# Sixteen-channel attention in a two-layer decoder: another order for the products of the row maximum

## The chip, the cores and the metric

The kernel runs on one core of one Trainium2 chip, as one program. The metric is the device time of one launch in microseconds (us), the median of three runs.

## The reference

The program is a whole two-layer decoder on x of shape (4, 512, 256), with a context of shape (4, 1601, 256). The change is in the second layer's cross attention alone: 16 heads of 16 channels, full softmax over 1601 keys, no mask.

```python
q = _split_heads(Q @ W_q.T + b_q)
k = _split_heads(K @ W_k.T + b_k)
v = _split_heads(V @ W_v.T + b_v)
scores = jnp.einsum('bhqd,bhkd->bhqk', q, k) / jnp.sqrt(jnp.float32(D_K))
probs = jax.nn.softmax(scores, axis=-1)
ctx = jnp.einsum('bhqk,bhkd->bhqd', probs, v)
```

## The kernel before

The function is `full_attention` (line 1577). One *unit* is a batch b and a group g of four heads, 16 units in all, numbered u = 4b + g. The four heads j of a group lie in four quarters of the partitions, 32 rows each (16 channels, one row for the maximum, the rest zero). So a product of head j uses only rows 32j to 32j+31 of TensorE's array, its *quarter*.

For each unit the softmax's maximum is found first. It takes 64 *chunks*: a chunk (line 1845) is one product of 128 queries by 400 keys of one head, written to one of three PSUM banks, the *ring*. VectorE reads it (line 1753) into one column of row maxima and so frees the bank (`ring_free`). After the last chunk `row_max` folds the columns and negates them into `less`; TensorE turns `less` (line 1852), VectorE adds it to the queries (`shift`, line 1766), so that the scores come out with the maximum taken off.

Then the unit is worked through in 13 *slots*, one for each tile of 128 keys. In slot s TensorE does, in its written order, the score products of tile s+1 (line 1866, one for each head, 512 queries wide, each waits until ScalarE has taken the bank's last exponential) and the *output* products of tile s (line 1877, four heads in four column strips). ScalarE does the exponentials (line 1715). The 64 chunks of the *next* unit are spread over slots 0 to 10 (`chunks_of`: 5, 6, 6, 6, 6, 5, 6, 6, 6, 6, 6). The first four of a slot are interleaved with the four score products (score 0, chunk, score 1, chunk, ...), the others follow. `chunk_at` gives chunk i the head i % 4. The sets thus begin on heads 0, 1, 3, 1, 3, 1, 2, 0, 2, 0, 2 in slots 0 to 10. So in slots 0, 7 and 9 every score product stands beside a chunk of its own head.

The ring also takes other work, in the order that `take` writes down and that all engines follow:
- a *piece*: one part of the next batch's Q, K or V (lines 1825 to 1832, two products over all 128 rows, each in two passes), taken by VectorE (lines 1741 to 1747). Each batch has 33, in slots 0 to 12 of the units with g = 1 and 2 and slots 0 to 6 of those with g = 3, for the first three batches. The piece stands after the slot's chunks and ahead of the output products.
- *sums*, in slot 1: the product that adds up and spreads the softmax's denominators of the unit before (line 1885). VectorE takes its reciprocal (line 1770) and scales the unit's output with it (line 1772).
- *out*, in slots 4 and 5 after the last group of a batch: the output projection (line 1894), added to x by VectorE (line 1777).

A TensorE instruction that needs a bank waits until the use three turns before has been read (`await_bank`).

Of the kernel before, what the change touches and what calls it, by code (L numbers as in the profile page):

```python
# [27 lines left out]
TB = T // P  # L28
S2 = 1601
KT = -(-S2 // P)  # L30
# [1516 lines left out]
FJ = P // FQ  # L1547
# [4 lines left out]
NKB = len(KB)  # L1552
# [24 lines left out]
def full_attention(nc, c):  # L1577
# [4 lines left out]
    SCALE = float(FD) ** -0.5  # L1582
    UNITS = [(b, g) for b in range(B) for g in range(FG)]
    LAST_UNIT = len(UNITS) - 1
    CHUNKS = FJ * TB * NKB
    MAX_SLOTS = KT - 2
    LESS_SLOT, SUMS_SLOT, OUT_SLOTS = KT - 2, 1, (4, 5)
    RING = 3
    with Scope(nc, "fa") as s:
# [48 lines left out]

        def chunks_of(slot):

            return range(CHUNKS * min(slot, MAX_SLOTS) // MAX_SLOTS, CHUNKS * min(slot + 1, MAX_SLOTS) // MAX_SLOTS)

        def first_chunks(n):

            rest = len(PIECES) - FIRST
            return range(CHUNKS * n // rest, CHUNKS * (n + 1) // rest)

        def chunk_at(i):

            return i % FJ, i // FJ // NKB, i // FJ % NKB  # L1650

        def piece_of(u, slot):

            b, g = UNITS[u]
            n = (g - 1) * KT + slot
            return n if b + 1 < B and g >= 1 and n < len(PIECES) else None
# [6 lines left out]
        def take(*use):  # L1663
            turn[use] = len(turn)
# [5 lines left out]
        take("less", 0)  # L1670
        for u, (b, g) in enumerate(UNITS):
            for slot in range(KT):
                for i in chunks_of(slot) if u < LAST_UNIT else ():
                    take("chunk", u + 1, i)
                if slot == LESS_SLOT and u < LAST_UNIT:
                    take("less", u + 1)
                if piece_of(u, slot) is not None:
                    take("piece", b + 1, piece_of(u, slot))
                if slot == SUMS_SLOT and u:
                    take("sums", u - 1)  # L1680
                if slot in OUT_SLOTS and u and ends(u - 1):
                    take("out", b - 1, OUT_SLOTS.index(slot))
# [47 lines left out]
        @block.vector  # L1730
        def _(dve):
            def await_turn(*use):
                dve.wait_ge(ring_ready, turn[use] + 1)

            def piece(b, n):
                what, g, m = PIECES[n]
                await_turn("piece", b, n)
                src = bank("piece", b, n)
                if what == "V":
                    rows = keys(m)  # L1740
                    ins = nc.vector.tensor_tensor(V[0:rows, b % 2, m, :, 0:FD], src[0:rows, 0:D].rearrange("p (h d) -> p h d", d=FD),
                                                  bv[0:rows, :].rearrange("p (h d) -> p h d", d=FD), ALU.add)
                elif what == "Q":
                    ins = nc.vector.tensor_scalar(Q[:, b % 2, g, :], src[:], bqk[:, 0, g:g + 1], None, ALU.add)
                else:
                    k0, w = KEYS[m]
                    ins = nc.vector.tensor_scalar(K[:, b % 2, g, k0:k0 + w], src[:, 0:w], bqk[:, 1, g:g + 1], None, ALU.add)
                ins.then_inc(ring_free, 1)

            def chunk(u, i):  # L1750
                j, t, n = chunk_at(i)
                await_turn("chunk", u, i)
                nc.vector.tensor_reduce(part[:, t, j, n:n + 1], bank("chunk", u, i)[:, 0:KB[n][1]], AX, ALU.max  # L1753
                                        ).then_inc(ring_free, 1)

            def row_max(u):
                dve.wait_ge(ring_free, turn["chunk", u, CHUNKS - 1] + 1)
                nc.vector.tensor_reduce(top[:].rearrange("p t j -> p (t j)"), part[:].rearrange("p t j n -> p (t j) n"), AX, ALU.max
                                        ).then_inc(top_ready, 1)
                dve.wait_ge(top_ready, u + 1)  # L1760
                nc.vector.tensor_scalar(less[:, :, :, DEN], top[:], -1.0, None, ALU.mult).then_inc(less_ready, 1)

            def shift(u):
                b, g = UNITS[u]
                await_turn("less", u)
                nc.vector.tensor_tensor(Qm[:, u % 2, :], bank("less", u)[:], Q[:, b % 2, g, :], ALU.add).then_inc(ring_free, 1)

            def scale(u):
                await_turn("sums", u)
                nc.vector.reciprocal(share[:], bank("sums", u)[:]).then_inc(ring_free, 1)  # L1770
                dve.wait_ge(ring_free, turn["sums", u] + 1)
                nc.vector.tensor_tensor(att[:, UNITS[u][1], :], raw[:], share[:], ALU.mult).then_inc(att_ready, 1)

            def add_output(b, half):
                rows = c.x[:, b * TB + half * 2:b * TB + half * 2 + 2, :]
                await_turn("out", b, half)
                nc.vector.tensor_tensor(rows, rows, bank("out", b, half)[:].rearrange("p (t d) -> p t d", d=D), ALU.add
                                        ).then_inc(ring_free, 1)

            nc.vector.memset(pv[:], 0.0).then_inc(made, 1)  # L1780
            dve.wait_ge(loaded, LOADS)
            dve.wait_ge(made, MADE)
            for n in range(len(PIECES)):
                piece(0, n)
                for i in first_chunks(n - FIRST) if n >= FIRST else ():
                    chunk(0, i)
            row_max(0)
            shift(0)
            dve.wait_ge(based, 1)
            for u, (b, g) in enumerate(UNITS):  # L1790
                for slot in range(KT):
                    if u < LAST_UNIT:
                        for i in chunks_of(slot):
                            chunk(u + 1, i)
                        if slot == MAX_SLOTS - 1:
                            row_max(u + 1)
                        if slot == LESS_SLOT:
                            shift(u + 1)
                    if piece_of(u, slot) is not None:
                        piece(b + 1, piece_of(u, slot))  # L1800
                    if slot == SUMS_SLOT and u:
                        scale(u - 1)
                    if slot in OUT_SLOTS and u and ends(u - 1):
                        add_output(b - 1, OUT_SLOTS.index(slot))
            scale(LAST_UNIT)
            for half in range(2):
                add_output(B - 1, half)

        @block.tensor
        def _(pe):  # L1810
# [45 lines left out]
            def scores(u, kt, j):  # L1856

                b, g = UNITS[u]
                n = keys(kt)
                at = (u * KT + kt) * FJ + j  # L1860
                if kt == 0 and j == 0:
                    pe.wait_ge(ring_free, turn["less", u] + 1)
                if at >= FJ:
                    pe.wait_ge(p_ready, at - FJ + 1)
                rows = slice(j * FQ, (j + 1) * FQ)
                nc.tensor.matmul(sps[j][0:n, :], K[rows, b % 2, g, kt * P:kt * P + n], Qm[rows, u % 2, :],  # L1866
                                 start=True, stop=True).then_inc(s_ready, 1)
# [38 lines left out]
                scores(0, 0, j)  # L1906
            for u, (b, g) in enumerate(UNITS):
                for slot in range(KT):
                    ahead = list(chunks_of(slot)) if u < LAST_UNIT else []
                    nxt = (u, slot + 1) if slot + 1 < KT else (u + 1, 0) if u < LAST_UNIT else None  # L1910
                    for j in range(FJ):
                        if nxt and nxt != (u + 1, 0):
                            scores(*nxt, j)
                        if j < len(ahead):
                            chunk(u + 1, ahead[j])
                    for i in ahead[FJ:]:
                        chunk(u + 1, i)
                    if slot == LESS_SLOT and u < LAST_UNIT:
                        turn_less(u + 1)
                    if piece_of(u, slot) is not None:  # L1920
                        piece(b + 1, piece_of(u, slot))
                    if nxt == (u + 1, 0):
                        for j in range(FJ):
                            scores(*nxt, j)
                    if slot == SUMS_SLOT and u:
                        add_up(u - 1)
                    if slot in OUT_SLOTS and u and ends(u - 1):
                        out_product(b - 1, OUT_SLOTS.index(slot))
                    output(u, slot)
            add_up(LAST_UNIT)  # L1930
            for half in range(2):
                out_product(B - 1, half)
# [1209 lines left out]
```

## Time and profile before

| | us |
|---|---|
| median of three runs | 8619.73 |
| lowest and highest | 8613.97, 8625.38 |
| profiled execution, device time | 8617.03 |
| its span | 8615.2 |
| main loop of `full_attention` in it | 1134.30 |
| TensorE busy in the loop | 1097.03 |
| VectorE, ScalarE busy in the loop | 635.78, 446.33 |

The span is the time from the first to the last instruction that the profiler saw; the device time lies 1.8 us above. Busy times of engines overlap. Products in different quarters run beside each other, and their ends are modelled, so a busy TensorE is not one at its limit.

### The profile page before, as it was taken

What the parts mean: (1) busy time and instruction counts of PE and PEld (TensorE: products, weight loads), DVE (VectorE), ACT (ScalarE), POOL (GpSimd) and SP (SyncE); (2) the same over time, 40 slices, a digit from 0 to 9 for tenths busy, and PEclk for the clock granted to TensorE, in tenths of its full rate; (3) what the DMA queues carried; (4) which work ended last, traced back from release to release, by engine and by line L of the source; (5) the groups of instructions that cost most, each with busy time, mean ns of one, the idle gap of its engine ahead of it and who ended that gap; (6) DMA issues with size and microseconds to landing.
All of it is one profiled execution on the core that took longest, in us unless ns stands there. A gap on an engine that the chain in (4) does not pass through costs nothing. (4 is left out here: it accounts for less than half of the span.)

```text
span 8615.2 us, 102487 instructions
## 1 busy us (share of the span) xinstructions
PE 7109.9 (83%) x35402; PEld 4802.5 (56%) x35402; DVE 4861.0 (56%) x7898; ACT 2854.5 (33%) x5165; POOL 711.7 (8%) x695
## 2 busy tenths in 40 slices
PE   6887887887879888888888889956653899999799
PEld 4775766756757666666666744422222334333577
DVE  5656655656646666666666610058886555555621
ACT  3223222232224444444444411134441233334210
POOL 0111111111100000000000000023333000000000
PEclk8998998998989999999999999978886899999895
DMA  0000000000000000000000010000000000000110
GB/s 33 0 1 1 0 1 1 0 1 1 0 33 9 7 20 9 7 20 7 8 19 9 7 55 0 0 18 0 0 0 3 26 8 1 8 1 1 40 49 10
DMA packets 23873, 89.02 MB, mean 10 GB/s; under 512 B 5784, under 2 KB 9120, under 8 KB 18480
## 3 DMA queue, kind: packets, MB, share of 16 engines
q1 hardware_dynamic: 23456, 83.53, 2.8%
q8 instruction: 253, 4.15, 0.2%
q14 instruction: 164, 1.34, 0.1%
HBM read 81.43 MB, written 2.10 MB: 10 GB/s over the span
## 5 line engine op out<-in xcount | busy, mean ns | idle before, releaser
L1252 DVE TENSOR_TENSOR xa_PT<-xa_tps,xa_PT 128x512 fp32r<-128x512 f32 (+1 forms) x1024 | 555.3, 584 | 386.0 <-ACT xa_PT L1127 382.3
L1753 DVE TENSOR_REDUCE fa_part<-fa_ring 128x1 f32<-128x400 f32 (+1 forms) x1024 | 533.0, 569 | 330.2 <-PE fa_ring L1845 312.3
L1715 ACT ACTIVATE fa_prob<-fa_sps 128x512 f32<-128x512 f32 (+1 forms) x832 | 439.9, 601 | 782.8 <-PE fa_sps L1866 774.1
L635 DVE TENSOR_TENSOR gdn_XX<-gdn_XX,gdn_wps 128x512 f32<-128x512 f32 (+1 forms) x768 | 477.2, 640 | 367.8 <-PE gdn_wps L799 360.1
L496 ACT ACTIVATE gdn_Y<-gdn_yps 128x256 f32<-128x256 f32 x768 | 295.2, 384 | 1051.6 <-PE gdn_yps L784 1045.2
L1405 PE MATMUL xa_tps<-ident,xa_prob 128*128 128x128 f32 (+1 forms) x3328 | 501.4, 284 | 162.3 <-DVE xa_PT L1252 161.6
L1845 PE MATMUL fa_ring<-fa_K,fa_Q 32*128 32x400 f32 (+1 forms) x2048 | 586.6, 546 | 36.7 <-DVE fa_part L1753 23.5
L1405 PEld LDWEIGHTS xa_tps<-ident,xa_prob 128*128 128x128 f32 (+1 forms) x3328 | 393.1, 143 | 388.6 <-DVE xa_PT L1252 317.7
L1127 ACT ACTIVATE xa_PT<-xa_tps 128x512 fp32r<-128x512 f32 (+1 forms) x1024 | 471.2, 514 | 416.1 <-PE xa_tps L1405 415.9
L796 PE MATMUL gdn_wps<-gdn_Y,gdn_XX 128*128 128x128 f32 x3072 | 601.2, 287 | 2.9
L1240 DVE CUSTOM_DVE_ANT_0 xa_prob<-xa_sps,xa_mask 128x1604 f32<-128x1604 f32 x256 | 467.4, 1826 | 130.0 <-PE xa_sps L1387 123.4
L796 PEld LDWEIGHTS gdn_wps<-gdn_Y,gdn_XX 128*128 128x128 f32 x3072 | 472.9, 196 | 67.4 <-issue 35.9
L1115 ACT ACTIVATE xa_prob<-xa_prob,xa_neg 128x1604 f32<-128x1604 f32 x256 | 418.2, 1634 | 268.2 <-DVE xa_neg L1243 268.1
L799 PE MATMUL gdn_wps<-gdn_XX,gdn_Y 128*128 128x128 f32 x2560 | 503.5, 279 | 0.0
L1387 PE MATMUL xa_sps<-xa_K,xa_Q 128*128 128x402 f32 x2048 | 466.7, 372 | 29.6 <-issue 16.9
L1423 PE MATMUL xa_pv<-xa_PT,xa_V 128*128 128x256 f32 (+1 forms) x3328 | 453.4, 292 | 11.1 <-DVE xa_PT L1252 11.1
L2042 PE MATMUL ffn_mid<-ffn_hid,ffn_h 128*128 128x512 f32 x1024 | 441.5, 593 | 9.7 <-DVE ffn_hid L2008 6.3
L1423 PEld LDWEIGHTS xa_pv<-xa_PT,xa_V 128*128 128x128 f32 (+1 forms) x3328 | 415.9, 189 | 49.2 <-issue 28.8
L2361 DVE TENSOR_TENSOR_SCAN scan_h<-scan_dA,scan_dBx 128x2048 f32<-128x2048 f32 x64 | 407.8, 6372 | 26.4 <-POOL scan_dBx L2235 20.2
L1387 PEld LDWEIGHTS xa_sps<-xa_K,xa_Q 128*128 128x128 f32 x2048 | 382.7, 198 | 45.1 <-issue 36.0
L799 PEld LDWEIGHTS gdn_wps<-gdn_XX,gdn_Y 128*128 128x128 f32 x2560 | 398.5, 196 | 0.0
L1845 PEld LDWEIGHTS fa_ring<-fa_K,fa_Q 32*128 32x128 f32 x2048 | 245.9, 187 | 270.9 <-DVE fa_part L1753 222.2
(424 smaller groups left out, 12365.8 us busy)
## 6 DMA issues: line engine op xcount, KB each, us to landing
xa_wqk<-in_xa_wqk SPq DMA_DIRECT2D x64, 256.0 KB, 2.6
moe_own_w<-in_moe_w SPq DMA_DIRECT2D x14, 1024.0 KB
ffn_h<-in_ffn_h SPq DMA_DIRECT2D x2, 4096.0 KB, 27.5
xa_ctxT<-in_ctxT SPq DMA_DIRECT2D x4, 1601.0 KB
fa_ctxT<-in_ctxT SPq DMA_DIRECT2D x4, 1601.0 KB
xa_mask<-in_mask SPq DMA_DIRECT2D x4, 802.0 KB, 9.0
ffn_w<-in_ffn_w SPq DMA_DIRECT2D x3, 1024.0 KB, 18.1
x<-in_x SPq DMA_DIRECT2D x1, 2048.0 KB
```

Of the source, the lines that this page charges most:

```text
L635: nc.vector.tensor_tensor(X[:, half, 0:n], X[:, half, 0:n], wps[half][:, 0:n], ALU.subtract).then_inc(X_ready, 1)
L796: last = nc.tensor.matmul(wps[half][:, 0, e, :], X[:, half, 1, e, :], Y[:, h, :], start=True, stop=True)
L799: last = nc.tensor.matmul(wps[half][:, 1, e, :], Y[:, h, :], X[:, half, 1, e, :], start=True, stop=True)
L1127: nc.scalar.activation(PT[0:n, u // 2 % NPT, 0, k0:k1, u % 2, :], turned_bank(u, g)[0:n, 0:k1 - k0, :], ACT.Copy).then_inc(t_hi, 1)
L1240: nc.vector.tensor_tensor_reduce(parts(prob[:, e, :]), sps[:, :, 0:SW], parts(mask[:, u % TB if masked else 0, :]), 1.0, -3.0e38, ALU.add, ...
L1252: nc.vector.tensor_tensor(PT[0:n, u // 2 % NPT, 1, k0:k1, u % 2, :], turned_bank(u, g)[0:n, 0:k1 - k0, :], PT[0:n, u // 2 % NPT, 0, k0:k1, ...
L1387: last = nc.tensor.matmul(sps[:, n, 0:SWW], Q[:, hh % 2, e, q * P:(q + 1) * P], k, start=(e == 0), stop=(e == 1))
L1405: last = nc.tensor.transpose(turned_bank(u, g)[0:n, kt - k0, :], prob[:, u % 2, kt * P:kt * P + n], c.ident[:])
L1423: nc.tensor.matmul(pv[0:MV, 0:2 * P], V[0:n, kt, hh].rearrange("p e d -> p (e d)"), PT[0:n, pair % NPT, part, kt].rearrange("p a q -> p (a ...
L1753: nc.vector.tensor_reduce(part[:, t, j, n:n + 1], bank("chunk", u, i)[:, 0:KB[n][1]], AX, ALU.max).then_inc(ring_free, 1)
L1845: nc.tensor.matmul(bank("chunk", u, i)[:, 0:w], Q[rows, b % 2, g, t * P:(t + 1) * P], K[rows, b % 2, g, k0:k0 + w], start=True, stop=True) ...
L2042: last = nc.tensor.matmul(mid[m % 2][:], w[n][:, k, m * P:(m + 1) * P], hid[e][:, k, :], start=(k == 0), stop=(k == MH - 1))
```

## The change

The 64 chunks of a unit are shared out in whole sets of four: `chunks_of` gives 4, 4, 8, 4, 8, 4, 8, 4, 8, 4, 8 chunks to slots 0 to 10, split in an early part (four) and a late part (four or none). `chunk_at` begins each set at head 2. In a slot with a late part TensorE's order becomes: scores and early chunks interleaved, `less`, piece, late chunks, sums or out, output. In a slot without one: scores and early chunks, `less`, piece, output, sums or out. VectorE and the order of the ring follow. The row maximum is taken after slot 10's late part.

```diff
+    QUADS = TB * NKB
+    CHUNKS = FJ * QUADS
...
         def chunks_of(slot):
-            return range(CHUNKS * min(slot, MAX_SLOTS) // MAX_SLOTS, CHUNKS * min(slot + 1, MAX_SLOTS) // MAX_SLOTS)
+            first, last = (QUADS * min(n, MAX_SLOTS) // MAX_SLOTS * FJ for n in (slot, slot + 1))
+            return range(first, min(first + FJ, last)), range(first + FJ, last)
...
         def chunk_at(i):
-            return i % FJ, i // FJ // NKB, i // FJ % NKB
+            return (i + FJ // 2) % FJ, i // FJ // NKB, i // FJ % NKB
...
@@ the ring's order (VectorE's loop is changed in the same way) @@
-                for i in chunks_of(slot) if u < LAST_UNIT else ():
+                early, late = chunks_of(slot) if u < LAST_UNIT else ((), ())
+                for i in early:
                     take("chunk", u + 1, i)
                 if slot == LESS_SLOT and u < LAST_UNIT:
                     take("less", u + 1)
                 if piece_of(u, slot) is not None:
                     take("piece", b + 1, piece_of(u, slot))
+                for i in late:
+                    take("chunk", u + 1, i)
...
@@ TensorE @@
-                    ahead = list(chunks_of(slot)) if u < LAST_UNIT else []
-                    nxt = (u, slot + 1) if slot + 1 < KT else (u + 1, 0) if u < LAST_UNIT else None
+                    early, late = chunks_of(slot) if u < LAST_UNIT else ((), ())
                     for j in range(FJ):
-                        if nxt and nxt != (u + 1, 0):
-                            scores(*nxt, j)
-                        if j < len(ahead):
-                            chunk(u + 1, ahead[j])
-                    for i in ahead[FJ:]:
-                        chunk(u + 1, i)
+                        if slot + 1 < KT:
+                            scores(u, slot + 1, j)
+                        if j < len(early):
+                            chunk(u + 1, early[j])
                     if slot == LESS_SLOT and u < LAST_UNIT:
                         turn_less(u + 1)
                     if piece_of(u, slot) is not None:
                         piece(b + 1, piece_of(u, slot))
-                    if nxt == (u + 1, 0):
+                    if slot + 1 == KT and u < LAST_UNIT:
                         for j in range(FJ):
-                            scores(*nxt, j)
+                            scores(u + 1, 0, j)
+                    if not late:
+                        output(u, slot)
+                    for i in late:
+                        chunk(u + 1, i)
                     if slot == SUMS_SLOT and u:
                         add_up(u - 1)
                     if slot in OUT_SLOTS and u and ends(u - 1):
                         out_product(b - 1, OUT_SLOTS.index(slot))
-                    output(u, slot)
+                    if late:
+                        output(u, slot)
```

## Rows read from the trace of the kernel before

**Rows 1.** Part 5 of the page: costliest groups; busy, mean of one, idle before.
```profile
L1845 PE MATMUL fa_ring<-fa_K,fa_Q 32*128 32x400 f32 (+1 forms) x2048 | 586.6, 546 | 36.7 <-DVE fa_part L1753 23.5
```

**Rows 2.** Windows: stretch, us, each engine's busy time, PEclk; the main loop.
```profile
6803.60:7937.90 1134.30, 1097.03 (x5826) 435.78 (x5830) 635.78 (x1140) 446.33 (x847) 0.00 (x0) 0.97 0.01 4
```

**Rows 3.** Waits in the loop: who for whom, us in total, times, longest.
```profile
PEld fa_ring L1845 <- DVE fa_part L1753: 212.6, 462, 1.3
...
PEld fa_pv L1877 <- ACT fa_prob L1715: 30.5, 51, 0.8
```

**Rows 4.** Windows: slots 3, 4, 5, 6 and 7 of unit 0.
```profile
6825.44:6830.28 4.84, 4.84 (x34) 1.76 (x30) 3.17 (x6) 2.17 (x4) 0.00 (x0) 1.00 0.01 3
6830.28:6835.07 4.79, 4.76 (x34) 1.99 (x30) 3.18 (x6) 2.06 (x4) 0.00 (x0) 1.00 0.00 0
6835.07:6839.42 4.35, 4.35 (x31) 1.46 (x27) 2.69 (x5) 2.17 (x4) 0.00 (x0) 1.00 0.00 0
6839.42:6844.06 4.64, 4.62 (x33) 1.95 (x29) 3.08 (x6) 2.06 (x4) 0.00 (x0) 1.00 0.00 0
6844.06:6849.33 5.27, 4.63 (x33) 1.77 (x29) 3.08 (x6) 2.17 (x4) 0.00 (x0) 1.00 0.00 0
```

**Rows 5.** Timeline: slot 6 of unit 4 (quarter 2), then slot 7's first read.
```profile
7144.75 0.18 PEld L1866 LDWEIGHTS fa_sps<-fa_Qm,fa_K 32*128 32x128 f32 x1 [0.85 <-issue]
...
7145.95 0.57 DVE L1753 TENSOR_REDUCE fa_part<-fa_ring 128x1 f32<-128x401 f32 x1 [1.39 <-PE fa_ring L1845]
7146.44 0.57 DVE L1753 TENSOR_REDUCE fa_part<-fa_ring 128x1 f32<-128x401 f32 x1
7146.58 0.29 PEld L1845 LDWEIGHTS fa_ring<-fa_K,fa_Q 32*128 32x128 f32 x2 [0.68 <-DVE fa_part L1753]
...
7147.54 0.29 PEld L1845 LDWEIGHTS fa_ring<-fa_K,fa_Q 32*128 32x128 f32 x2 [0.19 <-DVE fa_part L1753]
7147.55 0.57 DVE L1753 TENSOR_REDUCE fa_part<-fa_ring 128x1 f32<-128x400 f32 x1
7148.41 0.13 PEld L1877 LDWEIGHTS fa_pv<-fa_prob,fa_V 128*17 128x17 f32 x8 [0.57 <-ACT fa_prob L1715]
7149.39 0.33 PEld L1866 LDWEIGHTS fa_sps<-fa_Qm,fa_K 32*128 32x128 f32 x8 [0.85 <-issue]
...
7151.22 3.14 DVE L1753 TENSOR_REDUCE fa_part<-fa_ring 128x1 f32<-128x400 f32 x6 [2.13 <-PE fa_ring L1845]
```

**Rows 6.** Windows: six chunks on quarter 2 with a V, K, last-K piece.
```profile
7214.80:7220.50 5.70, 5.68 (x37) 2.63 (x33) 3.50 (x7) 2.06 (x4) 0.00 (x0) 1.00 0.00 0
7292.53:7299.08 6.55, 6.53 (x37) 2.63 (x33) 3.83 (x7) 2.06 (x4) 0.00 (x0) 1.00 0.00 0
7074.35:7079.58 5.23, 5.21 (x37) 2.48 (x33) 3.36 (x7) 2.07 (x4) 0.00 (x0) 1.00 0.00 0
```

**Rows 7.** Windows of slot 1 (units 4 and 5); timeline: reciprocal in unit 4, slot 2.
```profile
7109.43:7115.32 5.89, 5.88 (x36) 2.05 (x32) 4.05 (x7) 2.17 (x4) 0.00 (x0) 1.00 0.00 0
7181.17:7188.78 7.61, 7.61 (x40) 2.81 (x37) 4.81 (x8) 2.17 (x4) 0.00 (x0) 1.00 0.00 0
...
7114.44 3.36 DVE L1770 RECIPROCAL fa_share<-fa_ring 128x512 f32<-128x512 f32 x1 [0.48 <-PE fa_ring L1885]
7115.31 0.18 PEld L1866 LDWEIGHTS fa_sps<-fa_Qm,fa_K 32*128 32x128 f32 x1 [0.85 <-issue]
...
7117.85 0.60 PE L1845 MATMUL fa_ring<-fa_K,fa_Q 32*128 32x400 f32 x1 [0.74 <-DVE fa_share L1770]
```

**Rows 8.** Windows: slot 2 (units 5, 6), slots 7, 9 (unit 5), slots 2-3 (unit 13).
```profile
7188.78:7197.25 8.47, 7.64 (x38) 2.67 (x34) 6.90 (x9) 2.17 (x4) 0.00 (x0) 1.00 0.00 0
7265.34:7274.56 9.22, 8.39 (x38) 3.20 (x34) 6.58 (x9) 2.17 (x4) 0.00 (x0) 0.81 0.00 0
7220.50:7226.84 6.34, 5.70 (x38) 2.45 (x34) 3.50 (x7) 2.17 (x4) 0.00 (x0) 1.00 0.00 0
7232.54:7240.46 7.92, 7.28 (x38) 2.96 (x34) 3.53 (x7) 2.17 (x4) 0.00 (x0) 0.78 0.00 0
7785.93:7800.14 14.21, 13.38 (x63) 4.86 (x59) 9.32 (x14) 4.34 (x8) 0.00 (x0) 0.76 0.00 0
```

More of the change, by code:

```diff
@@ L1584, in full_attention @@
     LAST_UNIT = len(UNITS) - 1
-    CHUNKS = FJ * TB * NKB
+    QUADS = TB * NKB
+    CHUNKS = FJ * QUADS
     MAX_SLOTS = KT - 2
@@ L1791, in _ @@
                 for slot in range(KT):
-                    if u < LAST_UNIT:
-                        for i in chunks_of(slot):
-                            chunk(u + 1, i)
[L1795 to L1798, printed above, removed]
+                    early, late = chunks_of(slot) if u < LAST_UNIT else ((), ())
+                    for i in early:
+                        chunk(u + 1, i)
+                    if slot == LESS_SLOT and u < LAST_UNIT:
+                        shift(u + 1)
                     if piece_of(u, slot) is not None:
                         piece(b + 1, piece_of(u, slot))
+                    for i in late:
+                        chunk(u + 1, i)
+                    if slot == MAX_SLOTS - 1 and u < LAST_UNIT:
+                        row_max(u + 1)
                     if slot == SUMS_SLOT and u:
@@ L1908, in _ @@
                 for slot in range(KT):
-                    ahead = list(chunks_of(slot)) if u < LAST_UNIT else []
-                    nxt = (u, slot + 1) if slot + 1 < KT else (u + 1, 0) if u < LAST_UNIT else None
+                    early, late = chunks_of(slot) if u < LAST_UNIT else ((), ())
                     for j in range(FJ):
-                        if nxt and nxt != (u + 1, 0):
-                            scores(*nxt, j)
-                        if j < len(ahead):
-                            chunk(u + 1, ahead[j])
-                    for i in ahead[FJ:]:
-                        chunk(u + 1, i)
+                        if slot + 1 < KT:
+                            scores(u, slot + 1, j)
+                        if j < len(early):
+                            chunk(u + 1, early[j])
                     if slot == LESS_SLOT and u < LAST_UNIT:
@@ L1921, in _ @@
                         piece(b + 1, piece_of(u, slot))
-                    if nxt == (u + 1, 0):
+                    if slot + 1 == KT and u < LAST_UNIT:
                         for j in range(FJ):
-                            scores(*nxt, j)
+                            scores(u + 1, 0, j)
+                    if not late:
+                        output(u, slot)
+                    for i in late:
+                        chunk(u + 1, i)
                     if slot == SUMS_SLOT and u:
```

## The prediction

> **What bounds the kernel now.** I read the costliest groups first [rows 1]: the products for the maximum (L1845, "chunks") keep TensorE for 587 us. Most of them lie in the stage's main loop, 1134 us of the span at a clock of 0.97, with VectorE busy for 636 and ScalarE for 446 [rows 2]. All parts below are about that loop, since little else is edited. Its waits [rows 3] say who sets the pace: loads of chunks wait 213 us for a read (L1753) to free one of three banks, and the output products wait only 31 us for ScalarE. So neither TensorE's speed nor ScalarE's decides; it is the loop chunk, read, free bank, next chunk.
>
> A unit has 13 slots. I count slot s from its first score product (that of tile s+1) to the next slot's. [Rows 4] are slots 3 to 7 of unit 0, which have no pieces: six chunks that begin on quarter 1 take 4.84, on quarter 3 4.79, five on quarter 1 4.35, six on quarter 2 4.64, six on quarter 0 5.27. Each chunk less is 0.49 (4.84 less 4.35). Quarter 2 is the best start, quarter 0 the worst, as there score product and chunk of the same quarter stand side by side: the first read begins at 1.83 us (7151.22 less 7149.39) instead of 1.20 (7145.95 less 7144.75) [rows 5].
>
> **The slots of the new order.** Every set now begins on quarter 2. The set of the interleaved four is then exactly what slot 6 of unit 4 had [rows 5], and I build from that slot: reads at 1.20, 1.69 and, the fourth, 2.80; the fourth chunk at 1.83, 0.63 after the first read's start, as it needs its bank; its read 0.97 after it; output products 0.87 after the last chunk's start (7148.41 less 7147.54); next slot 0.98 after these. Three chunks thus cost 0.63 + 0.97 = 1.60 us, where reads alone would be 1.45.
> - Four chunks: 1.83 + 0.87 + 0.98 = 3.68 us. Slots 0, 1, 3, 5, 7, 9.
> - Eight chunks: fourth read 2.80, fifth 3.29, so the eighth chunk at 3.29 + 0.63 = 3.92, output at 4.78, total 5.76. Slots 2, 4, 6, 8, 10.
> A pair is 9.44 against 9.28 for two sixes on quarter 2: the uneven sets cost 0.16 a pair, the better start pays for it.
>
> **A unit without pieces**, change by slot: 0 (was five on quarter 0, 5.27 less one chunk, 4.79): -1.11. 3: -1.16. 4: +0.97. 5: -0.68. 6, 8, 10: +1.12 each. 7, 9: -1.59 each. Together -1.80. Slots 1 and 2 hold the sums: before, product of the sums, then output; now output, then product. Slot 1 was 5.89 [rows 7], becomes 3.68 + 1.05 (the product: 5.89 less 4.84) = 4.73, -1.16. But the reciprocal (3.36 us [rows 7]) began 0.87 before slot 2 (7114.44 against 7115.31) (1.16 after its product, which stood 1.05 + 0.98 before slot 2); the product now stands 1.05 before slot 2, so it begins 0.11 into the slot. It is 0.98 later; all that hangs on it in slot 2, the third chunk and the fourth score product behind it (at 7117.85 now), is 0.98 later too. Slot 2 at full clock was 6.56 (8.47 in unit 5 with a 1.91 piece [rows 8]), and two chunks more are 1.12: 8.66, +2.10. The unit comes to **-0.86 us**; 14 units (1 to 14) make -12.0. Unit 0 has no sums and a slow start: its slots by the same prices give -2.0. Unit 15 has no chunks: 0. The output projections in slots 4 and 5 keep their 3.65 us.
>
> **Pieces.** A piece added 1.06 (V), 1.91 (K of 512, Q) or 0.59 us (last K) to a six-chunk slot on quarter 2 (the windows less 4.64) [rows 6]. In four-chunk slots this stays. In eight-chunk slots the piece now stands after the fourth chunk: it can start at 2.70 (0.87 after a chunk), where the fifth chunk would have started at 2.32. So everything later is late by the piece's length and 0.38 more. 39 pieces are in such slots (five in each of units 1, 2, 5, 6, 9, 10, three in 3, 7, 11): +14.8. In slot 1 piece and sums no longer stand together; before that saved 0.2 us (7.61 [rows 7] for 5.89 + 1.91): nine units, +1.8. VectorE's reads of a piece lie beside TensorE. The row maximum after slot 10 comes 1.12 us later in a slot that is 1.12 longer: 0. The first units' chunks before the loop only change quarter by rotation: 0. ctxT's load has 70 us until it is wanted: 0.
>
> The Trainium skill has a rule that speaks against this change: "Changing tiling mode (not just tile) drains the TensorE" (TensorEngine Tiling (Array Packing), Key Properties). The trace agrees in that a product over all rows starts 0.87 us after a chunk where a chunk on another quarter starts 0.48 after it (two in 0.96, 7146.58 to 7147.54) [rows 5]; without the rule the 14.8 us above would be nought.
>
> At full clock the sum is -12.0 - 2.0 + 14.8 + 1.8 = **+2.6 us**.
>
> **The clock.** Asked slot by slot, the clock falls to its lower level (1.2 GHz) at 14 places in units 1 to 14, for a few us each; [rows 8] hold three of them and two slots without. Nine are in slot 2, after TensorE's pause for the reciprocal; five in slots 7 and 9, which begin on quarter 0 and leave TensorE idle for 0.64 us (6.34 less 5.70). Eleven are short: slot 2 with V 9.22 where 6.56 + 1.06 = 7.62 is due, slot 9 with V 7.92 where slot 7 has 6.34, 1.6 us each. Three are long (units 1, 13, 14): slots 2 and 3 of unit 13 take 14.21 for 6.56 + 4.84, 2.8 us. Together 26 us, 8 of them in slots 7 and 9. Those five should go: -8. In slot 2 the pause before the third chunk grows from 0.74 [rows 7] to 1.7 us. In the five units there without a piece (4, 8, 12, 13, 14) it fell each time (3 x 1.6 + 2 x 2.8 = 10.4); I expect that again with one more of the long kind: 11.6. In the nine with a piece it fell in four (3 x 1.6 + 2.8 = 7.6); I expect five: 9.2. So +3. Bounds: it falls nowhere, -26 in all; in slot 2 of all 14 units at 2.8 us, 39 in place of 26, +13. Estimate: **-5 us**.
>
> In all 2.6 - 5 = -2 us. The profiled execution took 8617.03 (span 8615.2 and 1.8 around it): 8615 by it. The median of three is 8619.73, 2.7 above, so I say **8618 us**.
>
> **Rivals.**
> 1. *Clock falls in the sets of eight* (ends slower). From 1.83 to 4.78 us of such a slot TensorE does one chunk after another, each on a quarter of its rows, longer than now (1.83 to 3.66). If that is thin enough for the clock to fall, each fall costs 1.6 us; there are 75 such slots, 36 of them without a piece between. One in three of the 75: 25 x 1.6 = 40, 8658 us. It decides from 12 falls on (19 us on the -2). For it: slots 7 and 9 fell with three chunks after a pause. Against: they had a 0.65 us standstill, the new ones have none, and no slot on quarter 2 fell. 12%.
> 2. *Later reciprocal lowers the clock in every unit*: the bound above, +13, and +2.6: +16; with 0.6 us more in each where the slow stretch reaches further into slot 3, +24: 8635 to 8643. 8%.
> 3. *Falls nearly all go*, since no slot has same-quarter neighbours and the sets are denser: -26 + 2.6 = -23, 8596. Against it: the longer pause in slot 2. 9%.
> 4. *The mode change is paid on both sides of a split-off piece*: another 14.8 us on the -2, 8633. Against: V's 1.06 us in a slot already holds its way out into another mode [rows 6]. By the skill's rule on the mode this would be the drain back into the quarters. 4%.
> 5. *The change doesn't do what it says*: neighbours used other quarters already in slots 2, 4, 6, 8 and 10, so little is left to win; that is in the sum, and if the gain of 1.59 us in slots 7 and 9 did not come, 14 x 3.2 = 45 us slower. The rows of both starts stand side by side, so 2%.
>
> **How the numbers follow.** My forecast has 65%, the rivals 35%. Its own range is 8606 to 8630: the clock term by 8 us either way and the slot prices by 0.03 us over 154 slots, some 5 us. With rivals the range is 8596 to 8643. By 0.2% (17 us, about what a measurement tells from none): faster, below 8602.5, rival 3 and a tail: 0.12. Slower, above 8637, rivals 1 and 5, part of 2 and a tail: 0.18. Within: 0.70.
>
> **What would show it.** Four-chunk slots without a piece at 3.68 us and eight-chunk ones at 5.76; slot 8 with V 7.20 and with K 8.05; the reciprocal beginning 0.1 us inside slot 2 and slot 2 at 8.7 us or, with a fallen clock, near 10; stage within 10 us of 1134; clock full in slots 7 and 9 of units 1, 5, 9. Wrong if eight-chunk slots show a clock below 1, or if they take over 6.2 us at full clock.

## The result: 0.6% slower, and the profile after

The changed kernel takes 8675.29 us (8671.07 to 8678.64, 4 runs) against 8622.56 us for the kernel before in the same runs. The ratio is 1.0063, 95% interval 1.0047 to 1.0078. The forecast was 8618 us with a range of 8596 to 8643 us, so it was wrong, and on the side of rivals 1 and 2. One execution of a later experiment, e5_filler (10431 us), and one of the kernel before beside it (12307 us) ran at a lower clock from end to end and are left out of every median and ratio below.

In the code of after, chunks are at L1852, their reads at L1758, score products at L1873 and the reciprocal at L1775. The group of part 5 that answers to [rows 1]; its products are the same 2048, and 109 us longer:

```profile
L1852 PE MATMUL fa_ring<-fa_K,fa_Q 32*128 32x400 f32 (+1 forms) x2048 | 695.8, 581 | 30.1 <-DVE fa_share L1775 24.1
```

Waits in the loop, as [rows 3]. Chunks wait less for a free bank than before (175 for 213 us), so the waits for a bank, on which the prediction built, are not what grew:

```profile
PEld fa_ring L1852 <- DVE fa_part L1758: 174.8, 345, 1.3
```

Windows of after (stretch, us, busy PE, PEld, DVE, ACT, POOL, then PEclk): the loop, answering to [rows 2], and units 1 to 14; slots 7 and 8 of unit 7 (four and eight chunks); slot 8 of unit 5 (eight, V) and of unit 6 (eight, K), answering to [rows 6]; slots 1, 2 and 3 of unit 4 [rows 7]; slot 9 of unit 5 [rows 8]; slot 10 of unit 13.

```profile
6812.40:7995.30 1182.90, 1152.16 (x5806) 455.72 (x5806) 641.08 (x1140) 435.26 (x841) 0.00 (x0) 0.92 0.01 4
6875.19:7963.00 1087.81, 1057.95 (x5284) 420.60 (x5280) 602.58 (x1071) 384.30 (x744) 0.00 (x0) 0.92 0.01 4
7415.03:7418.71 3.68, 3.66 (x28) 1.37 (x24) 2.11 (x4) 2.06 (x4) 0.00 (x0) 1.00 0.61 255
7418.71:7424.48 5.77, 5.75 (x36) 2.54 (x32) 4.14 (x8) 2.06 (x4) 0.00 (x0) 1.00 0.00 0
7254.40:7261.61 7.21, 7.11 (x40) 2.93 (x36) 4.65 (x9) 2.06 (x4) 0.00 (x0) 1.00 0.01 2
7335.98:7344.04 8.06, 8.04 (x40) 2.94 (x36) 4.98 (x9) 2.06 (x4) 0.00 (x0) 1.00 0.00 0
7126.85:7131.58 4.73, 4.71 (x30) 1.67 (x26) 2.11 (x4) 2.07 (x4) 0.00 (x0) 1.00 0.00 0
7131.58:7142.62 11.04, 9.24 (x33) 3.57 (x32) 8.09 (x10) 2.17 (x4) 0.00 (x0) 0.72 0.00 0
7142.62:7147.82 5.20, 5.20 (x28) 2.33 (x24) 2.21 (x4) 2.17 (x4) 0.00 (x0) 0.62 0.00 0
7261.61:7266.35 4.74, 4.72 (x32) 2.05 (x28) 2.54 (x5) 2.07 (x4) 0.00 (x0) 1.00 0.00 0
7889.29:7895.91 6.62, 6.60 (x36) 2.56 (x32) 4.54 (x10) 2.06 (x4) 0.00 (x0) 0.87 0.00 0
```

Two things are to be seen. Where PEclk is 1.00 the slots have the lengths that were forecast: 3.68, 5.77 (for 5.76), 7.21 (7.20), 8.06 (8.05), 4.73. And the loop's clock is 0.92 where it was 0.97: slots 2 and 3 of unit 4 are at 0.72 and 0.62, and slot 10 of unit 13, eight chunks without a piece, takes 6.62 at 0.87. The prediction had named a clock below 1 in such a slot as a sign that it is wrong. There TensorE does one chunk after another and then the output products, which take 1.91 us where those of the slot before took 1.05:

```profile
7888.33 1.05 PE L1884 MATMUL fa_pv<-fa_prob,fa_V 128*17 128x512 f32 x8
...
7890.61 3.55 PE L1852 MATMUL fa_ring<-fa_K,fa_Q 32*128 32x400 f32 x11
7894.09 1.91 PE L1884 MATMUL fa_pv<-fa_prob,fa_V 128*17 128x512 f32 x8
```

The window of the loop (its first line above, 1182.90 us) ends where the last tile's score products start; to that point the loop of the kernel before took 1130.7 us. So it grew by 52 us, as much as the medians differ (53). The two profiled executions differ by 60 us; the other 8 lie ahead of the loop, in code that is the same in both. Slot 2 of unit 4 in the timeline (start, us, engine, line):

```profile
7131.71 3.36 DVE L1775 RECIPROCAL fa_share<-fa_ring 128x512 f32<-128x512 f32 x1 [1.47 <-PE fa_ring L1892]
...
7135.13 0.60 PE L1852 MATMUL fa_ring<-fa_K,fa_Q 32*128 32x400 f32 x1 [1.72 <-DVE fa_share L1775]
...
7136.34 1.03 PE L1852 MATMUL fa_ring<-fa_K,fa_Q 32*128 32x400 f32 x1
```

The reciprocal begins 0.13 us into the slot (forecast 0.11), TensorE stands still for 1.72 us for it (0.74 before, [rows 7]), and 1.2 us later a pass of a chunk (each product is done in two) takes 1.03 us in place of 0.60: the lower level of the clock.

### The profile page after: what moved, and what is told of

The parts are those of the page before. It is cut to its first block and busy times, and to the rows that moved or that the text cites. A ratio compares the mean times of both kernels' runs of the same rounds, so it can differ in the third digit from the quotient of the medians.

```text
span 8675.6 us, 102487 instructions
## 1 busy us (share of the span) xinstructions
PE 7171.4 (83%) x35402; PEld 4821.7 (56%) x35402; DVE 4867.6 (56%) x7898; ACT 2846.4 (33%) x5165; POOL 710.8 (8%) x695
## 5 line engine op out<-in xcount | busy, mean ns | idle before, releaser
L1758 DVE TENSOR_REDUCE fa_part<-fa_ring 128x1 f32<-128x400 f32 (+1 forms) x1024 | 538.3, 570 | 343.6 <-PE fa_ring L1852 327.1
L1852 PE MATMUL fa_ring<-fa_K,fa_Q 32*128 32x400 f32 (+1 forms) x2048 | 695.8, 581 | 30.1 <-DVE fa_share L1775 24.1
L1387 PE MATMUL xa_sps<-xa_K,xa_Q 128*128 128x402 f32 x2048 | 465.1, 371 | 29.6 <-issue 16.9
L1852 PEld LDWEIGHTS fa_ring<-fa_K,fa_Q 32*128 32x128 f32 x2048 | 270.2, 198 | 262.6 <-DVE fa_part L1758 184.4
L1873 PE MATMUL fa_sps<-fa_Qm,fa_K 32*128 32x512 f32 (+1 forms) x1664 | 412.6, 668 | 1.5 <-DVE fa_Qm L1771 0.8
## 6 DMA issues: line engine op xcount, KB each, us to landing
moe_own_w<-in_moe_w SPq DMA_DIRECT2D x14, 1024.0 KB
ffn_w<-in_ffn_w SPq DMA_DIRECT2D x3, 1024.0 KB, 18.1
```

The lines of the kernel that those rows point to most:

```text
L1387: last = nc.tensor.matmul(sps[:, n, 0:SWW], Q[:, hh % 2, e, q * P:(q + 1) * P], k, start=(e == 0), stop=(e == 1))
L1852: nc.tensor.matmul(bank("chunk", u, i)[:, 0:w], Q[rows, b % 2, g, t * P:(t + 1) * P], K[rows, b % 2, g, k0:k0 + w], start=True, stop=True) ...
```

## How each kernel is split into slots and clock

For units 1 to 14, a *full-clock sum* can be made for every kernel from the slot prices of the prediction: 154 slots, plus slots 11 and 12 as they are (2.59 and 2.65 without a piece). What the measured stretch has above it is what the clock cost. I split that into slots 2 and 3 and the rest, and count the places where the clock falls, by the slot in which it falls. "Still" is TensorE's standstill in slot 2, "behind" the chunks that follow it there one by one before the output (in the five units without a piece; with one, after and e1 have one chunk, the piece and then four), "most" the largest set in slots 4 to 10. Full-clock sums, clock and falls are for units 1 to 14 of the one profiled execution of each kernel. That of e5 is the fastest of its runs (8607.01 us), that of e9 the slowest (8541.42). Still, what the stretch gains or loses against the kernel before agrees with the ratios within 10 us.

| kernel | ratio to before (95%) | units 1-14 | full clock | clock, slots 2-3 | clock, rest | falls slot 2 / rest | still, behind, most |
|---|---|---|---|---|---|---|---|
| before | 1 | 1035.5 | 1008.5 | 18.8 | 8.2 | 9 / 5 | 0.74, 3, 6 |
| after | 1.0063 (1.0047-1.0078) | 1087.8 | 1013.1 | 49.9 | 24.9 | 14 / 12 | 1.72, 5, 8 |
| e1_sums_first | 1.0029 (1.0019-1.0040) | 1067.6 | 997.5 | 40.5 | 29.6 | 12 / 13 | 0.74, 5, 8 |
| e2_before_sums_late | 1.0038 (1.0024-1.0051) | 1068.9 | 1024.0 | 36.8 | 8.1 | 14 / 5 | 1.72, 3, 6 |
| e3_quarter_two | 0.9948 (0.9935-0.9962) | 993.8 | 971.6 | 21.9 | 0.3 | 9 / 0 | 0.74, 3, 6 |
| e4_piece_last | 1.0023 (1.0014-1.0032) | 1057.5 | 982.7 | 40.5 | 34.3 | 14 / 19 | 0.74, 5, 8 |
| e5_filler | 1.0003 (0.9994-1.0013) | 1033.8 | 1013.1 | 4.8 | 16.0 | 3 / 10 | filled, 5, 8 |
| e6_q2_filler | 0.9925 (0.9912-0.9938) | 971.9 | 971.6 | 0.0 | 0.2 | 0 / 0 | filled, 3, 6 |
| e7_sevens | 0.9987 (0.9979-0.9996) | 1033.1 | 980.6 | 35.2 | 17.3 | 13 / 10 | 0.74, 4, 7 |
| e8_slot2_four | 0.9939 (0.9927-0.9952) | 988.2 | 971.6 | 16.4 | 0.3 | 8 / 0 | 0.74, 1, 6 |
| e9_split | 0.9884 (0.9868-0.9901) | 945.0 | 944.7 | 0.1 | 0.2 | 0 / 0 | none, -, 6 |

In unit 0, which the table leaves out, the clock falls in slots 2, 6 and 10 of after, e1, e4 and e5. The others have no fall in it after the low clock with which every kernel's loop begins. (The 21 falls of e4 that the expectation of e7 names take in those of slots 6 and 10.)

e6 and e9, in which the clock never falls, meet their sums within 0.3 us in 972 and 945: the prices can be trusted to split the others.

The window of units 1 to 14 of the kernel before, against which the fences below are read:

```profile
6866.51:7902.00 1035.49, 1000.41 (x5286) 400.48 (x5282) 597.28 (x1071) 391.64 (x744) 0.00 (x0) 0.97 0.01 4
```

## The experiments

Theory A: the reciprocal begins later, TensorE stands still longer in slot 2, the clock falls. Theory B: the sets of eight lower it, chunk after chunk, each on a quarter of the rows. Of kernels e1 to e4 the lines shown are units 1 to 14.

**e1_sums_first**: after, with the sums' product ahead of the output again.

```diff
-                    if not late:
+                    if not late and slot != SUMS_SLOT:
                         output(u, slot)
...
-                    if late:
+                    if late or slot == SUMS_SLOT:
                         output(u, slot)
```

> The changed kernel with one edit taken back: in slot 1 the product of the sums stands ahead of the output products again. Full-clock prices of its slots against the kernel before: +4.6 us (the changed kernel) - 14 x 0.98 (reciprocal earlier) - 1.8 (piece and sums together again) = -11. Theory A (the reciprocal that begins 0.98 us later lengthens TensorE's pause in slot 2, and that lowers the clock there): the clock's cost goes back to about that of the kernel before less its 8 us in slots 7 and 9, so 8600 to 8612 us, and slots 2 and 3 together lose under 25 us to the clock instead of 50. Theory B (the sets of eight, chunk after chunk on a quarter of the rows, are what lowers it): the clock still costs 35 us or more above the kernel before, 8640 to 8655 us.

8643.69 us (8640.02 to 8653.13, before 8615.47).

```profile
6870.17:7937.81 1067.64, 1051.07 (x5286) 418.09 (x5282) 602.78 (x1071) 384.39 (x744) 0.00 (x0) 0.92 0.01 4
```

In units 1 to 14 it wins back 20 us, and 15.6 of them are slot prices. The clock still costs 70 us, and 12 falls stay in slot 2: theory B's figure. By the ratios e1 is 29 us faster than after, so the later reciprocal is 5 us (these two traces) to 14 us (the ratios) of the clock's cost, a small part as long as the sets of eight stand.

**e2_before_sums_late**: before, with that edit alone.

```diff
-                    if slot == SUMS_SLOT and u:
-                        add_up(u - 1)
+                    if slot == SUMS_SLOT:
+                        output(u, slot)
+                        if u:
+                            add_up(u - 1)
```

> The kernel before with this one edit done alone: in slot 1 the output products stand ahead of the product of the sums. Full-clock prices: 14 x 0.98 + 1.8 = +15.5 us. Theory A: the clock falls in slot 2 of nearly all 14 units and costs 15 to 25 us more, 8650 to 8663 us. Theory B: the clock costs what it did, 8635 to 8640 us.

8650.78 us (8643.80 to 8654.58).

```profile
6862.13:7931.03 1068.90, 1020.58 (x5286) 409.26 (x5282) 597.86 (x1071) 391.66 (x744) 0.00 (x0) 0.95 0.01 4
```

The full-clock sum is 15.5 us more, the clock costs 18 us more in slots 2 and 3, and it falls there in all 14 units: theory A. So the later sums lower the clock without sets of eight, and the sets of eight lower it without the later sums (e1). The two overlap in slot 2.

**e3_quarter_two**: before, sets of five and six kept, each begun on head 2.

```diff
+        HEADS, rest = [], 0
+        for slot in range(MAX_SLOTS):
+            n = len(chunks_of(slot))
+            HEADS += [(k + FJ // 2) % FJ for k in range(FJ)] + [(rest + k + FJ // 2) % FJ for k in range(n - FJ)]
+            rest += n - FJ
+        NTH = [HEADS[:i].count(j) for i, j in enumerate(HEADS)]
         def chunk_at(i):
-            return i % FJ, i // FJ // NKB, i // FJ % NKB
+            return HEADS[i], NTH[i] // NKB, NTH[i] % NKB
```

> The kernel before with its five or six chunks a slot, only the heads of each slot's set are chosen so that every set begins on head 2. Nothing else is moved. Both theories have the full-clock prices -2.44 us a unit (slots 0, 7, 9: -0.63; 1, 3, 5: -0.20; 4: -0.15), about -37 us. If the falls in slots 7 and 9 came from same-quarter neighbours, 8 us more: 8575 to 8582 us. If they came from the number of chunks in a row instead, they stay or move: 8585 to 8595 us.

8570.38 us (8563.20 to 8582.78).

```profile
6861.21:7855.02 993.81, 979.88 (x5286) 410.75 (x5282) 593.59 (x1071) 383.22 (x744) 0.00 (x0) 0.98 0.01 4
```

This is below the range of 8575 to 8582 us, on the side of the same-quarter neighbours: 45 us less than the 8615.47 of the kernel before here, the sum of the expectation's 37 and 8. The five falls in slots 7 and 9 are gone, and with them 8 us; the order of the quarters is worth 37 us more (2.64 us a unit, which the expectation's terms give too; it summed them wrongly to 2.44). The order by head, a part of the change, is good. What came with it is not.

**e4_piece_last**: e1, with the piece behind the late chunks again.

```diff
+                for i in late:
+                    take("chunk", u + 1, i)
                 if piece_of(u, slot) is not None:
                     take("piece", b + 1, piece_of(u, slot))
-                for i in late:
-                    take("chunk", u + 1, i)
```

(and so on VectorE and TensorE)

> As e1_sums_first, and the piece stands after the late chunks again, right ahead of the output. Full-clock prices: -11 - 39 x 0.38 = -26 us. Theory A: the clock as in e1, 8585 to 8600 us. Theory B: eight chunks in a row now stand in all 75 slots without a piece between, the clock falls more often, 8630 us or above.

8636.90 us (8625.58 to 8658.48).

```profile
6869.16:7926.66 1057.50, 1043.65 (x5286) 427.49 (x5282) 600.34 (x1071) 383.72 (x744) 0.00 (x0) 0.92 0.01 4
```

The window is 10.1 us shorter than e1's where the prices say 14.8. The price itself is right: slot 8 of unit 6, eight chunks with a K piece behind them, takes 7.68 us at full clock, the 5.76 of the chunks and the 1.91 of the piece, where after took 8.06. A third of what is won goes back into the clock (19 falls outside slot 2 for 13). It is not shown that the piece between the chunks had kept the clock up. Falls in sets with a piece go from 5 to 8 (of 30), but in sets without one, which this edit leaves as they are, from 8 to 11 (of 26).

**e5_filler**: after, with TensorE's standstill filled.

```diff
+                        if u and slot == SUMS_SLOT + 1 and j == 2 and u < LAST_UNIT:
+                            fill(u, slot + 1)
...
+            def fill(u, kt):
+                pe.wait_ge(p_ready, (u * KT + kt) * FJ)
+                for _ in range(2):
+                    nc.tensor.matmul(sps[FJ - 1][:], sums[:], c.xnT[:, 0, 0:T], start=True, stop=True)
```

> The changed kernel with two products more, over all rows and 512 columns, in slot 2 of units 1 to 14, between the third score product and the third chunk, where TensorE stands still until the reciprocal is done. They go to the bank of the fourth score product, which overwrites them, so nothing of the result changes. Theory A (the standstill lowers the clock): the 14 falls in slot 2 are gone or nearly, 35 us less than the changed kernel, about 8640 us. Theory B (chunk after chunk on a quarter of the rows lowers it, and in slot 2 six such chunks follow the standstill): the clock still falls in slot 2 of the five units without a piece there, in 10 or more of all 14, and the falls in slots 4, 6, 8 and 10 stay; 8655 us or above.

8619.70 us, against 8618.86 for the kernel before in the same runs: by the ratios 0.6% less than after, some 52 us. Slot 2 of unit 13 and of unit 5:

```profile
7780.13:7788.79 8.66, 8.66 (x39) 3.25 (x38) 8.09 (x10) 2.17 (x4) 0.00 (x0) 1.00 0.01 2
...
7177.46:7188.42 10.96, 10.96 (x44) 3.64 (x44) 8.93 (x11) 2.18 (x4) 0.00 (x0) 1.00 0.00 0
```

Work was added, two products a unit, 28 in all, and the kernel is faster by more than both theories gave. Slot 2 has its forecast full-clock length, 8.66 and 10.96 (10.95), with the reciprocal as late as in after. So what after loses there above its full-clock price was the clock's and not the wait's. Three falls stay in slot 2, some 8 us into it, far behind the standstill; the ten in slots 4, 8 and 10, all in sets of eight without a piece, are theory B's.

**e6_q2_filler**: e3 with one such product a unit (`fill` as above, one pass of its loop).

```diff
+                        if u and slot == SUMS_SLOT + 1 and j == 2 and u < LAST_UNIT:
+                            fill(u, slot + 1)
                         if j < len(ahead):
                             chunk(u + 1, ahead[j])
```

> e3_quarter_two with one such product more in the same place (the standstill there is 0.74 us). In e3 the clock fell 9 times, all in slot 2, which cost about 19 us. Both theories: with the standstill filled and only three chunks in a row behind it the falls are gone, at most 0.5 us a unit is lost to the product itself: 8552 to 8560 us. If filling leaves them, the chunks in a row are enough by themselves: 8570 to 8578 us.

8553.06 us (8549.30 to 8555.79).

```profile
6867.67:7839.54 971.87, 969.55 (x5312) 408.74 (x5308) 593.57 (x1071) 383.22 (x744) 0.00 (x0) 1.00 0.01 4
```

No fall is left, as expected. The product itself costs nothing that can be seen: it lies in a wait that is as long as before (slot 2 without a piece stays 6.56 us).

**e7_sevens**: e3 with other sizes (the heads of the tails are picked so that no neighbours share a quarter).

```diff
+    SIZES = (5, 6, 7, 5, 7, 5, 7, 5, 7, 5, 5)
...
-            return range(CHUNKS * min(slot, MAX_SLOTS) // MAX_SLOTS, CHUNKS * min(slot + 1, MAX_SLOTS) // MAX_SLOTS)
+            return range(sum(SIZES[:slot]), sum(SIZES[:slot + 1]))
```

> e3_quarter_two with other sizes of the sets, 5, 6, 7, 5, 7, 5, 7, 5, 7, 5, 5 chunks in slots 0 to 10, all begun on head 2 and no neighbours on one quarter. Full-clock prices: a seventh chunk costs 0.64 us and a chunk less saves 0.48, about +7 us on e3. Theory B: in sets of seven the clock falls less often than in the 75 sets of eight of e4 (21 falls there outside slot 2) and more often than in e3's sixes (none), so 3 to 12 falls outside slot 2: 8582 to 8600 us. Theory A: none outside slot 2, 8577 us.

8609.13 us (8596.90 to 8622.21): slower than the range of either theory. Slot 2 had a seventh chunk too, which the expectation left out: slots 2 and 3 lose 35.2 us to the clock, 13 more than in e3.

```profile
6867.82:7900.93 1033.11, 1019.29 (x5284) 420.40 (x5280) 597.63 (x1071) 383.65 (x744) 0.00 (x0) 0.94 0.01 4
```

There are 10 falls outside slot 2, all in sets of seven, between the none of sets of six and the 19 of sets of eight. They come with no standstill at all: slot 8 of unit 4 is busy for 5.87 of its 5.89 us, at a clock of 0.89. More chunks in a row bring more falls there.

**e8_slot2_four**: e3 with `SIZES = (6, 6, 4, 6, 6, 6, 6, 6, 6, 6, 6)`.

> e3_quarter_two with 6, 6, 4, 6, 6, 6, 6, 6, 6, 6, 6 chunks: two fewer in slot 2, the standstill for the reciprocal as it was. Full-clock prices: 0. Theory B: with one chunk instead of three behind the standstill the nine falls in slot 2 are gone: 8552 us. Theory A: the standstill alone is enough, they stay: 8570 us.

8567.53 us (8556.79 to 8570.58), not told apart from e3. Slot 2 of units 11 (Q piece) and 12:

```profile
7613.11:7623.91 10.80, 9.98 (x36) 2.77 (x32) 5.93 (x7) 2.17 (x4) 0.00 (x0) 0.68 0.01 2
...
7682.94:7688.53 5.59, 4.77 (x31) 1.40 (x27) 5.18 (x6) 2.17 (x4) 0.00 (x0) 1.00 0.00 0
```

Theory B's 8552 us is not met, theory A's 8570 is: eight falls stay with only one chunk behind the standstill. Of the five units without a piece one still falls (e3: two), of the nine with one the same seven as in e3. Three chunks in a row behind the standstill were not what kept the nine falls of e3 alive.

**e9_split**: e3 with the standstill taken away and nothing added in its place. VectorE copies the sums out of the bank and takes the reciprocal in four parts.

```diff
+    LESS_SLOT, SUMS_SLOT, OUT_SLOTS, PARTS = KT - 2, 1, (6, 7), 4
...
-                nc.vector.reciprocal(share[:], bank("sums", u)[:]).then_inc(ring_free, 1)
-                dve.wait_ge(ring_free, turn["sums", u] + 1)
-                nc.vector.tensor_tensor(att[:, UNITS[u][1], :], raw[:], share[:], ALU.mult).then_inc(att_ready, 1)
+                nc.vector.tensor_copy(share[:], bank("sums", u)[:]).then_inc(ring_free, 1)
...
+            def scale_part(u, k):
+                w = slice(k * T // PARTS, (k + 1) * T // PARTS)
+                if k == 0:
+                    dve.wait_ge(ring_free, turn["sums", u] + 1)
+                nc.vector.reciprocal(share[:, w], share[:, w]).then_inc(shared_out, 1)
+                dve.wait_ge(shared_out, u * PARTS + k + 1)
+                nc.vector.tensor_tensor(att[:, UNITS[u][1], w], raw[:, w], share[:, w], ALU.mult).then_inc(att_ready, 1)
...
+                    if u and SUMS_SLOT < slot <= SUMS_SLOT + PARTS:
+                        scale_part(u - 1, slot - SUMS_SLOT - 1)
```

> e3_quarter_two with the standstill of slot 2 taken away: VectorE copies the product of the sums out of its bank in slot 1, and does the reciprocal and the scaling in four parts of 128 columns at the starts of slots 2 to 5, where it has no chunk to read yet; the output projections go to slots 6 and 7 instead of 4 and 5. If the clock falls in slot 2 because TensorE stands still there for the reciprocal, no fall is left in units 1 to 14 (-19 us on e3), and slot 2 at full clock goes from 6.56 to 4.64 us, -27 more: 8523 to 8530 us. If the chunks in a row or the change of mode are what lowers it, falls remain: 8540 us or above.

8520.63 us (8506.93 to 8541.42) against 8615.64: 1.2% faster than the kernel before, the best of all, and just below the 8523 to 8530 us expected. VectorE in slots 1 and 2 of unit 12:

```profile
7657.34 3.14 DVE L1761 TENSOR_REDUCE fa_part<-fa_ring 128x1 f32<-128x400 f32 x6 [1.50 <-PE fa_ring L1863]
7660.96 0.69 DVE L1778 COPY fa_share<-fa_ring 128x512 f32<-128x512 f32 x1 [0.48 <-PE fa_ring L1903]
7661.69 0.95 DVE L1784 RECIPROCAL fa_share<-fa_share 128x128 f32<-128x128 f32 x1
7662.67 0.29 DVE L1786 TENSOR_TENSOR fa_att<-fa_raw,fa_share 128x128 f32<-128x128 f32 x1
7663.03 3.33 DVE L1761 TENSOR_REDUCE fa_part<-fa_ring 128x1 f32<-128x400 f32 x6
7666.28 0.94 DVE L1784 RECIPROCAL fa_share<-fa_share 128x128 f32<-128x128 f32 x1
```

The parts lie in the 1.5 us that VectorE has free at the head of a slot, the reads go on at once, and units 1 to 14 run at full clock, though TensorE got no product more. This is shown for sets of five and six alone; no run takes the standstill away from a kernel with sets of eight:

```profile
6880.70:7825.73 945.03, 942.44 (x5284) 404.37 (x5280) 613.30 (x1169) 381.73 (x744) 0.00 (x0) 1.00 0.01 4
```

## Why the prediction was wrong

**Slots of four and eight, right.** 3.68 and 5.76 us were built from one slot's timeline and measured as 3.68 and 5.77. So were slot 1 (4.73) and the reciprocal's place.

**Pieces, right.** 7.21 and 8.06 for 7.20 and 8.05. The 0.38 us for a piece that splits the chunks held, and rival 4, a second such price, is out. e4 is the test: with the piece behind all eight chunks the slot with K takes 7.68 us in place of 8.06. The Trainium skill says "Changing tiling mode (not just tile) drains the TensorE" (TensorEngine Tiling (Array Packing), Key Properties). The traces agree, as far as one such price for each split piece goes.

**The full-clock sum, right for units 1 to 14.** Forecast -12.0 + 14.8 + 1.8 = +4.6 us, by the slots of after +4.6 (1013.1 less 1008.5). The slots that after and e5, which share their order, show at full clock add up to 1013.3. Unit 0, forecast at -2.0, came to -0.1 (62.8 for 62.9): the clock fell three times in its sets of eight.

**The clock, the step that failed.** "Estimate: -5 us" was +48 (27 us before, 75 after, units 1 to 14). The prediction put it together from three parts.
- "Those five should go: -8" was right: no fall in slots 7 and 9, slot 9 of unit 5 is 4.74 at 1.00.
- Slot 2, forecast at +3, was +31. I let the falls be 10 and they were 14, all units; and I let a long one cost 2.8, where the mean of after is 49.9 / 14 = 3.6. That was even above my bound of 39. Two things did it, and they overlap: the longer standstill (0.74 to 1.72) alone gives +18 (e2), the sets of eight without it +22 (e1), both +31. This is rival 2, held at 8%: the clock fell in slot 2 of every unit, and without the falls in slots 4 to 10 it would have cost 23 us more than before, where that rival had 13 to 21.
- Slots 4 to 10, forecast at nothing, have 12 falls and 25 us, where the kernel before had 8 us in slots 7 and 9. This is rival 1, held at 12%, with 2.1 us a fall for its 1.6, and fewer falls than its 25: with unit 0 there are 15 beside those of slot 2 in units 1 to 14.

Of the 53 us by which the clock term missed, 28 are slot 2's and 25 those of slots 4 to 10. Two rivals came true together, and the prediction had no case for both at once.

The prediction treated the clock as something that a standstill does. The row that I took as evidence against rival 1, that no slot on quarter 2 fell, was from sets of six only; e7 shows that one chunk more already brings falls. Rows of sets of six alone say nothing of longer sets, and the range should have had the 40 us of rival 1 inside it.

**Which is shown and which is not.** Shown: filling the standstill of after takes 45 of its 50 us in slots 2 and 3 away and brings the kernel back to 1.0003 (e5); with more chunks in a row there are more falls elsewhere (e3 none, e7 10, e4 19). In after 8 of those 12 falls are in the 26 sets without a piece and 4 in the 30 with one, all four with the short last K piece. Standstill and chunks in slot 2 act together. The clock's cost in slots 2 and 3, by the standstill and the chunks behind it as in the table, is 16 us (0.74, 1), 19 to 22 (0.74, 3), 35 (0.74, 4), 40 (0.74, 5), 37 (1.72, 3), 50 (1.72, 5). Open: why a fall in slot 2 costs 1.6 us in one unit and over 3 in another. In after the clock falls 3.1 to 6.1 us into slot 2, and no run sets that place. Open too is what a split-off piece does for the clock, and how the falls vary from one execution to the next, as each kernel has one trace.

## What to carry to other kernels

Where the granted clock is near full but not full, price a new order twice, at full clock and by what it does to the dense stretches: here the full-clock sum was right within 2 us and the result was over 50 us away. Where products that use few rows follow each other one by one, keep such a stretch no longer than the longest that your traces show at full clock, or test the longer one first. Of an edit with several parts, run the parts alone: here the order of the quarters gives -0.5%, grouping into fours and eights takes 0.8% back (e4 against e3), and a wait that both versions carry, the whole reciprocal out of one bank, was worth 0.6% more (e9 against e3).

## What the runs showed of the hardware

A TensorE that is busy all the time can still lose its clock. In slot 10 of unit 13 of after it is busy for 6.60 of 6.62 us, and the granted clock is 0.87: before it fell the engine did one chunk after another, each on 32 of its 128 rows. The Trainium skill describes the clock gate as a block that "watches PE busy-ness and gates its clock" (TensorE: Matmul & The Clock Gate, Terms); the busy share of the profile did not tell here whether the clock would hold.

Added work can pay. The 14 products over all rows in e6 fill a standstill of 0.74 us a unit. They keep the clock at 1.00 and take 22 us off e3's units 1 to 14; by the medians the kernel is 17 us faster.
